# Early key groups of the relu pass, a ring of four key chunks, and another order at the kernel's start

## The reference

```
x = x + softmax(split(LN(x) Wq) split(ctx Wk)^T / 8) split(ctx Wv) Wo + bo       # 16 heads of 64
x = x + banded_attention(LN(x))                                                   # 16 heads of 16
x = x + experts(LN(x), 8 experts of 512, 2 chosen)
q = relu(LN(x) W^T + b);  k = relu(ctx W^T + b)
x = x + softmax(masked(q k^T)) k                                                  # one head of 256
x = x + scan(LN(x))
x = x + experts(LN(x), 32 experts of 128, 8 chosen, and a shared one)
```

## Time and profile before

| what | us |
|---|---|
| median of 3 runs | 1545.11 |
| lowest, highest | 1542.7, 1546.9 |
| the profiled execution | 1538.79 |
| its span on the core | 1537.1 |
| PE busy | 1453.0 |
| DVE busy | 1089.3 |
| ACT busy | 829.3 |
| POOL busy | 606.7 |

### The profile page before, as it was taken

One profiled execution on the slowest core, in us unless ns is written; L12 is line 12 of the kernel. 1 busy time (PEld: TensorE's weight loads), 2 busy tenths in 40 slices (PEclk: granted clock), 3 DMA queues, 4 the chain that ended last, 5 costly groups with the idle time before them and its releaser, 6 DMA issues. The chain is left out here.

```text
span 1537.1 us, 24554 instructions
## 1 busy us (share of the span) xinstructions
PE 1453.0 (95%) x9077; PEld 1254.4 (82%) x9077; DVE 1089.3 (71%) x2052; ACT 829.3 (54%) x1578; POOL 606.7 (39%) x519
## 2 busy tenths in 40 slices
PE   6999999999999999999999999999986879999479
PEld 5888888888888888888888888888875769999248
DVE  6777777777777777777777777777786337777774
ACT  2656655565565655656656566555652236666221
POOL 6343443434343434343434343343300245776240
PEclk9999999999999999999999999999998799999689
DMA  5000000000000000000000000000005121221720
GB/s 185 1 3 23 1 25 1 25 1 25 1 25 1 25 1 25 1 25 1 25 1 22 5 1 25 1 1 1 1 28 205 56 105 55 81 82 35 316 88 4
DMA packets 11098, 58.90 MB, mean 38 GB/s; under 512 B 2330, under 2 KB 4707, under 8 KB 9956
## 3 DMA queue, kind: packets, MB, share of 16 engines
q1 hardware_dynamic: 10980, 57.33, 10.0%
HBM read 57.19 MB, written 0.13 MB: 37 GB/s over the span
## 5 line engine op out<-in xcount | busy, mean ns | idle before, releaser
L471 DVE TENSOR_TENSOR pT<-ps,pT 128x896 fp32r<-128x896 f32 x224 | 244.4, 1091 | 203.8 <-ACT pT L381 203.8
L308 POOL CAST V<-Vraw 128x512 fp32r<-128x512 f32 x189 | 115.7, 612 | 653.3 <-ACT Vraw L387 552.7
L381 ACT ACTIVATE pT<-ps 128x896 fp32r<-128x896 f32 x224 | 206.0, 919 | 179.4 <-PE ps L543 178.6
L387 ACT COPY Vraw<-ps 128x512 f32<-128x512 f32 x189 | 110.9, 587 | 266.0 <-PE ps L525 266.0
L309 POOL TENSOR_TENSOR V<-Vraw,V 128x512 fp32r<-128x512 f32 x189 | 242.7, 1284 | 15.1
L425 DVE TENSOR_REDUCE nmx<-ps 128x1 f32<-128x896 f32 x224 | 241.9, 1080 | 0.0
L368 ACT ACTIVATE prob<-ps,nm 128x896 f32<-128x896 f32 x224 | 223.8, 999 | 0.0
L601 PE MATMUL ps<-ident,prob 128*128 128x128 f32 x1568 | 214.2, 277 | 8.7 <-ACT prob L368 4.5
L556 PEld LDWEIGHTS ps<-pT,V 128*128 128x128 f32 x1568 | 214.9, 188 | 8.1 <-issue 0.3
L556 PE MATMUL ps<-pT,V 128*128 128x256 f32 x1568 | 220.3, 280 | 0.0
L601 PEld LDWEIGHTS ps<-ident,prob 128*128 128x128 f32 x1568 | 167.5, 140 | 17.0 <-ACT prob L368 9.2
(11 more groups left out here) (304 smaller groups left out, 2403.5 us busy)
## 6 DMA issues: line engine op xcount, KB each, us to landing
raw<-in_ctxT SPq DMA_DIRECT2D x14, 896.0 KB, 4.4
d_raw<-in_ctxT SPq DMA_DIRECT2D x14, 896.0 KB, 4.7
w<-in_w SPq DMA_DIRECT2D x2, 4096.0 KB, 17.9
wg<-in_wg SPq DMA_DIRECT2D x1, 4352.0 KB, 17.2
wu<-in_wu SPq DMA_DIRECT2D x1, 4352.0 KB, 27.0
wd<-in_wd SPq DMA_DIRECT2D x1, 4352.0 KB, 37.5
e_ea<-in_alog SPq DMA_DIRECT2D x1, 2048.0 KB, 7.3
d_mrow<-in_mask SPq DMA_DIRECT2D x14, 112.0 KB, 4.6
```

What stands on the lines that cost most here:

```text
L308: link(pool, nc.gpsimd.tensor_copy(v_high(g, i), by_head(Vraw[:, j % 2, :])), "pool_chain")
L381: nc.scalar.activation(pT[u % 2][:, :, 0, :], pT_ps, ACT.Copy).then_inc(sem("pTh_ready"), 1)
L471: nc.vector.tensor_tensor(pT[u % 2][:, :, 1, :], pT_ps, pT[u % 2][:, :, 0, :].bitcast(F32), ALU.subtract).then_inc(sem("pTl_ready"), 1)
```

## The change

Twelve of the 56 key groups are made ahead of the relu pass. `later_at` places groups 0 to 5 in steps 216, 217, 218, 219, 222 and 223 of the large pass, where the values would stand; groups 6 and 7 follow the first half of the output projection and the turning of heads; groups 8 and 9 stand in the band behind its scores; groups 10 and 11 at the head of the first expert stage. For the first eight the large pass splits two more context chunks (chunks 0 and 1 again, as the fifteenth and sixteenth), the last of them when the last piece is done. For the other four the band loads chunks 2 and 3, and ACT and POOL split them there. `d_kT` becomes a ring of four chunks. The weights of the relu pass are loaded and split at the kernel's start; their split and that of chunk 0 leave the first expert stage. Some constants are made by POOL in the band and no more at the start. In the relu pass `done` begins at 15, and rows of the first chunk are turned ahead of group 14.

At the kernel's start the first context chunk is loaded first and is split by ACT and DVE, as are the left halves of the key and value weights, and two pieces stand ahead of the query projection. In a piece the matmul with the low context now precedes that with the low weight.

```
+    later_at = [steps - 8, steps - 7, steps - 6, steps - 5, steps - 2, steps - 1]
 large pass, PE:
+                def later_keys(G, bank):
+                    c = chunks + G // LG
+                    if G == 0:
+                        pe.wait_ge(sem("wx_split"), 1)
+                    if G % LG == 0:
+                        pe.wait_ge(sem("cT_split"), 2 * c + 2)
+                    if 0 < G < len(later_at):
+                        pe.wait_ge(sem("dkT_ready"), G)
+                    relu_keys(nc, v, G % LG, cTh[c % 2], cTl[c % 2], ps[:, bank, 0:HK]).then_inc(sem("dk_done"), 1)
...
+                    if u in later_at:
+                        pe.wait_ge(sem("o_added"), u - 1)
+                        pe.wait_ge(sem("vraw_ready"), len(v_steps))
+                        later_keys(later_at.index(u), 6)
 large pass, ACT, ahead of exp_step(u + 1):
+                    if u in later_at:
+                        later_keys(later_at.index(u), 6)
 large pass, POOL:
-                    elif u % H0 == H0 - 2 and u // H0 + 2 < chunks:
+                    elif u % H0 == H0 - 2:
                         split_context(u // H0 + 2)
+                split_context(chunks + 1)
 band, POOL:
                 norm_pool(pool, 1)
+                nc.gpsimd.iota(...) x2, affine_select(tri), memset(below), affine_select(below)
+                later_low(nc, pool, sem, v, 0)
                 pool.wait_ge(sem("s1_max"), 1)
                 nc.gpsimd.tensor_tensor(part(s, 0), ...).then_inc(sem("s1_shifted0"), 1)
+                later_low(nc, pool, sem, v, 1)
 relu pass:
-    done = [max(early, ahead)]
+    early, done = 12, [15]
...
 relu pass, ACT:
+                for n in range(3):
+                    rows_high(0, n)
                 for G in range(before, done[0]):
                     keys(G)
+                rows_high(0, 3)
                 for C in to_split[0]:
                     split_high(C)
-                for n in range(NG):
-                    rows_high(0, n)
                 exp_step(0)
+def later_low(nc, pool, sem, v, i):
+
+    pool.wait_ge(sem("dcTh_ready"), i + 1)
+    nc.gpsimd.tensor_tensor(v["d_cTl"][i][:, :, :], v["d_raw"][i][:, :, :], v["d_cTh"][i][:, :, :].bitcast(F32),
+                            ALU.subtract).then_inc(sem("dcTl_ready"), 1)
```

More of the change, by code:

```diff
@@ L84, in build @@
         keep("row0", [P, P])
-        keep("tri", [P, P])
         keep("hmask", [P, HPT])
-        keep("below", [P, E1, E1])
-        keep("disti", [P, 2, P], I32)
-        keep("dist", [P, P])
         keep("brow", [1, 3 * D])
-        for name in ("aq", "ak", "av", "afc"):
+        for name in ("aq", "ak", "av"):
             keep(name, [P, KT, D])
@@ L123, in build @@
         norms = (norm_vector, norm_pool, norm_tensor)
+        keep("bx", [P, KT])
+        keep("d_wxh", [P, KT, D], F32R)
+        keep("d_wxl", [P, KT, D], F32R)
+        v["d_kT"] = [sb(f"d_kT{i}", [P, KT, CK]) for i in range(2)]
         stage_context(nc, t, sb, sem, link, ps, norms, v)
+        keep("tri", [P, P])
+        keep("below", [P, E1, E1])
+        keep("disti", [P, 2, P], I32)
+        keep("dist", [P, P])
+        keep("afc", [P, KT, D])
+        keep("wx", [P, KT, D])
         keep("wg0", [P, KT, E0])
@@ L142, in build @@
                 v["d_cTl"] = [sb(f"d_cTl{i}", [P, KT, CK], F32R, second) for i in range(2)]
[L143 to L145 removed]
+                v["d_kT"] += [sb(f"d_kT{i}", [P, KT, CK], F32, second) for i in range(2, 4)]
                 with ExitStack() as first:
@@ L292, in split_context, with split_weight @@
                                             ALU.subtract).then_inc(sem("cT_split"), 1)
[L294 to L298, removed]
+                def split_weight(w, high, low, arrived, split):
+                    pool.wait_ge(sem(arrived), 32)
+                    link(pool, nc.gpsimd.tensor_copy(high[:, :, right], w[:, :, right]), "pool_chain")
+                    nc.gpsimd.tensor_tensor(low[:, :, right], w[:, :, right], high[:, :, right].bitcast(F32),
+                                            ALU.subtract).then_inc(sem(split), 1)
                 def split_values(j):
@@ L848, in stage_scan @@
         inv = [sb(f"e_inv{i}", [P, W], F32, own) for i in range(2)]
-        g = [sb(f"e_g{i}", [P, W], F32, own) for i in range(2)]
+        g = [x[:, :, :].rearrange("p k n -> p (k n)")[:, 0:W] for x in v["d_kT"][0:2]]
         def cn(x):
@@ L1044, in stage_relu_context @@
     groups = KG * chunks
-    early, split = v["early_groups"], v["early_splits"]
-    ahead = v["groups_ahead"]
-    done = [max(early, ahead)]
+    early, done = 12, [15]
+    SKIP = 2
     for c in range(chunks):
@@ L1055, in first_use @@
         return next((c for c in range(chunks) if done[c + 1] > KG * C), None)
-    to_split = {c: [C for C in range(chunks) if KG * C >= done[0] and max(first_use(C) - 1, 0) == c]
-                for c in range(chunks)}
+    to_split = {c: [C for C in range(2 + SKIP, chunks) if max(first_use(C) - 1, 0) == c] for c in range(chunks)}
     with ExitStack() as own:
@@ L1136, in _ @@
                 norm_pool(pool, 3)
-                for C in range(split, (done[0] + KG - 1) // KG):
-                    split_low(C)
                 for g in range(KG):
@@ L1180, in exp_step @@
                                          accum_out=rs[:, b:b + 1]).then_inc(sem("dexp_done"), 1)
-                act.wait_ge(sem("wx_in"), 32)
-                for C in range(split, (done[0] + KG - 1) // KG):
-                    split_high(C)
                 before = min(early + 2, done[0])
```

259 lines of the change are left out of this document (154 added, 105 removed).

## The result

| | us |
|---|---|
| before, median of 19 runs | 1541.65 (1538.48 to 1546.90) |
| after, median of 19 runs | 1548.58 (1546.77 to 1551.51) |
| ratio, 95% interval | 1.0044 (1.0035 to 1.0054) |
| span of the profiled execution | 1545.4, before 1537.1 |

The change costs 6.9 us, 0.44%. The predicted 1548.0 is close to the measured 1548.58, but not for the reasons given: the sum said +2.95, and the two profiles differ by +8.3. The 1548.0 started from the 1545.11 of three runs; the median of 19 is 3.5 us lower, and that happened to cover most of the error of the sum, which is 4.0 us in the medians. That the total came out is luck.

The account below looks back on a forecast made before the run. PE's own queue was taken as the bound wherever it shows no idle time. Terms -2.0 + 5.75 + 3.6 + 1 + 5.9 + 0 - 0.6 - 10.7 = +2.95 on 1545.1 gave 1548.0 us, range 1537 to 1555.

Parts of the forecast that it names:

- The start: Kernel start: first context arriving first and two pieces ahead of the query projection bring the first scores sooner, -2.0 us.
- Pairs 216 to 219: End of the large pass: two groups in each pair of steps mostly fill PE's holes, costing 1.4 us, bounds 0 and 4.9.
- The lock at the scaling: End of the large pass: POOL's 4 us split of the sixteenth context blocks DVE's scaling of heads, +3.6 us.
- the clock behind the hole: Large pass: the 5 us hole from the blocked scaling may leave PE at its lower clock, +1 us, bounds 0 and 2.
- The tail, groups 4 to 7: Large pass end: +0.9 for step 222's group, 2.5 for groups 5 and 6, 0.95 for group 7.
- The band: POOL's low halves block DVE's mask (+2.4) and second shift (+3.5), +5.9 us; the two groups there cost nothing.
- The lock at the shift: Band: POOL goes straight into the other low half and blocks DVE's shift of the second half, +3.5 us.
- The first expert stage: Two groups lie in the hole ahead of a turning; 0 us, bounds -2 and +2.
- The relu pass up to T(0): Relu pass start to its first turning of probabilities, paced by POOL's low halves and key parts: -0.6, bounds -3 and +1.
- The relu loop: Eleven iterations with three groups instead of four take 11.5 us instead of 12.47, held by DVE and POOL: -10.7 us.
- the bound if PE alone decides: Relu loop: each of eleven iterations gains 1.24 us if only PE sets the pace, -13.6 us.
- the three rivals: Locks off the path, 1537.6, 0.22; relu loop paced by POOL and DVE, 1553.3, 0.20; lower clock doubles early groups, 1550.5, 0.13.

Follow-up runs that it names:

- kernel 2: Changed kernel, with POOL's low half of the sixteenth context waiting until DVE has scaled the fifth pair of heads; 1544.03 us.
- kernel 9: kernel 8 with groups 4 to 7 each cut to one matmul of two columns, their keys not computed; 1525.29 us.
- kernel 3: Changed kernel, with POOL's low half of context chunk 3 in the band waiting for DVE's masked output weights; 1543.98 us.
- Kernel 6: kernel 5 with both POOL low halves behind the masked output weights, groups 8, 9 moved to the first expert stage, 10, 11 to the relu pass; 1530.23 us.
- kernel 5: Changed kernel with the edits of kernel 1, kernel 2 and kernel 3, and POOL's constants tri and below made behind both low halves; 1532.03 us.
- kernel 4: Kernel before, with high weight by low context second and low weight by high context third in a piece of keys; 1544.31 us.
- kernel 11: Kernel before with only the new start of the large pass: load order, splits by ACT and DVE, two pieces ahead of the query projection; 1538.88 us.
- kernel 10: kernel 8 with group 5 in step 223 put in bank 7, so PE skips the wait for its rectification; 1525.32 us.
- kernel 7: kernel 5 with chunk 4's high half earlier on ACT and chunk 5's low half later on POOL at the relu pass start; 1529.58 us.
- kernel 1: Changed kernel, with SP issuing each mask one context load earlier in the relu pass; 1540.72 us.
- kernel 8: Kernel 6 with the reordered relu pass start of kernel 7, so all edits together; 1524.80 us.

## Why the prediction was right or wrong

**The start: right in kind, -2.9 (first turning of probabilities) for -2.0.** The query projection behind the two pieces took 3.73 us where 4.4 were assumed; the clock granted in it was 1.00. Of the 1.3 us more that came over the steps 0 to 216 the prediction says nothing.

**Pairs 216 to 219: +0.7 for +1.4,** read as the change of the turning of step 216 to that of step 220. Inside the bounds.

**The lock at the scaling: right.** +3.7 for +3.6, and kernel 2 shows that DVE's own length was its cause. +1.5 for +1 by the clock behind the hole, but kernel 2 has nearly the same loss at step 222 without the hole: as an effect of that hole it isn't shown. The Trainium skill (SBUF — State Buffer, section Who interferes with whom) calls it an exclusive lock on the ports that DVE and GpSimd share, and has the order of issue decide who blocks. By that rule 0.1 us decides about 3.7, and the trace agrees: POOL starts 0.1 us ahead of DVE in the changed kernel and 0.4 behind it in kernel 2.

**The tail, groups 4 to 7: +4.7 for +4.35** (0.7 between the turnings of steps 222 and 223, 4.0 behind them). The size was right and the working wrong, so that part is luck. A wait was overlooked: PE doesn't apply the probabilities until ACT has rectified the group, 0.72 us in steps 222 and 223. And kernel 9 shows that the groups don't count by their length, as the prediction has it: without their work the tail is 1.6 us shorter and not 4.9, and the same time is measured for the whole.

**The band: +10.4 for +5.9. Here a step failed by its size.** The lock at the shift gave +3.35 for +3.5, and kernel 3 shows it. The queries came 2.5 us later, as forecast with 2.4, but by two locks: 1.7 of it is the mask, and 0.8 was left out, POOL's constant `below` (L1659) holding DVE's `b_flu` for 1.10 us instead of 0.16. Left out too was the clock: the scores L1774 took 5.40 us and the products L1790 6.85, where they had taken 3.76 and 3.77, at granted clocks of 0.68 and 0.50 against 1.00 and 0.95. On the path that is 1.5 and 3.1 us. The terms 2.5, 1.5, 3.35 and 3.1 add up to the 10.4. By their own length the two groups did cost nothing, as the prediction says: PE still waits 1.27 us behind them. Kernel 6, with groups and low halves gone from the band's chain, has scores and products at granted clocks of 1.00 and 0.93 and a band of 33.4 us. What sets the clock in the products stays open: kernel 3 excludes the length of PE's last hole, and kernel 5 has groups, late mask and long scores without the half clock. Of the 1.5 for the scores much may be chance, since kernels 4 and 11 differ from the kernel before by 1.7 us in a band of the same code.

**The first expert stage: right,** -0.9 for 0, inside its bounds. In kernels 2, 6, 9 and 10, where its first 48 matmuls ran at a granted clock of 0.79, it took 38.7 us.

**The relu pass up to T(0): -1.5 for -0.6,** inside the bounds. Its time was set by POOL's two halves in a row, as the prediction has it, but not only through what stands behind them on POOL: they held DVE's four casts too, 9.79 us where kernel 7 has 3.18. Kernel 7 took 4.2 us from it.

**The relu loop: -6.0 for -10.7. This is the step that failed by its reasoning.** The iteration was taken as 11.5 us, for DVE and POOL; it takes 11.19 to 11.35, PE's own 11.2, and a distance of 11.2 is what the prediction itself named as a sign of being wrong. That part gives -13.8 (-14.0 in kernel 1), where -13.6 was named as the bound if PE alone decides. Against it stand 7.8 us by a wait that the prediction doesn't contain. It counted PE, ACT, DVE and POOL, and not SP. A mask stands on SP behind a context load, and that load waits until the chunk two before it is split. Before, the mask of chunk c stood behind the load of chunk c + 2. The new condition puts it behind the load of chunk c + 4, and so behind the split of chunk c + 2. With three groups an iteration the split of chunk 11 falls into iteration 8, the very one in which the scores of chunk 9 are masked. This could have been read from the table `done` and the diff. None of the three rivals is this one. Kernel 1 shows it: one condition, and 18.97 becomes 11.20.

**What follows, and the median.** Behind T(13) the instructions are the same in all kernels, and the profiles show 112.6 to 112.7 us in five of them and 114.8 to 115.9 in the other eight. It goes with the clock: from 50 to 70 us behind T(13) the granted clock is 0.84 and then 0.75 in the changed kernel (112.6) and 0.63 and then 0.52 in kernel 1 (115.9). The profiled execution before was one of the short ones, and fits with its lying under the median; among the 35 executions of the kernel before that were measured with kernels 1 to 4, those of 1538.7 to 1539.6 us have a mean granted clock of 0.976 or 0.977 and those of 1547.2 to 1547.8 one of 0.972. So a difference of two single profiles is uncertain by some 3 us even where the stages in question agree to 0.1.

## What to carry to other kernels

When work is moved from a loop into earlier holes, go through each queue, the one that issues DMAs too, and list what every wait on it holds up. A load that waits for a split also holds up everything that stands behind it on its queue; here that was a mask, and the iteration that made the split was the one that needed it. Where a POOL instruction of 4 us with SBUF inputs comes near a DVE operation with two SBUF inputs, or a copy or tensor_scalar in SBUF, put a semaphore between them, so that DVE goes first; here such waits and moves, together with one mask, turned +0.44% into -1.1%. Don't price matrix work at the border of two stages by its length: leaving out 4.9 us of it gained nothing. And don't read a difference of 1 or 2 us in a short stage from one profile of each kernel.

## What the runs showed of the hardware

- The granted clock in short stages differs between profiles of the same code. The first 48 matmuls of the first expert stage took 5.60 us at 1.00 in the changed kernel, 1, 3, 5, 7 and 8, and 6.97 to 7.01 at 0.79 in 2, 6, 9 and 10, so that kernels 6 and 8, alike up to there, differ by 1.8 us in this stage. Behind a wait of 2.62 us in both, five pairs of group matmuls ahead of T(0) take 0.79 to 0.95 us each in kernel 8 (granted 0.54) and 0.57 to 0.68 in kernel 10, and T(0) comes 1.4 us later.
- DVE beside a POOL subtraction of 4 us: a reduction from SBUF (2.46 us for two), a reciprocal of 128x16 (0.25) and a copy from PSUM (1.22) keep their lengths; a copy in SBUF (four casts 9.79 for 3.2), tensor_scalar over 128x128 (3.43 for 0.29), a multiplication of two SBUF inputs (4.02 for 0.29) and a scalar_tensor_tensor over 128x2 (1.10 for 0.16, beside an affine_select) don't.
